# Attention with windows of three blocks: TensorE's step in another order (one piece for the q and k projection, the turned blocks in two pairs)

## The reference

```
qkv = xn @ Wqkv + bqkv            # 16 heads of 32, blocks of 128 tokens
scores = q @ kwin.T * 512 ** -0.5 # kwin: own block, the one before, the one behind
mask: |kpos - qpos| <= 128, and inside the sequence
attn = softmax(scores); out = attn @ vwin
x + out @ Wout + bout + ffn(xn)
```

## Time and profile before

| | before |
|---|---|
| median of 3 runs | 2508.47 us (2508.38 to 2508.74) |
| profiled execution | 2504.68 us |
| its span | 2502.9 us |
| PE busy | 2440.0 us, 97% |
| PEld, DVE, ACT, POOL busy | 80%, 64%, 58%, 14% |
| mean granted clock | 0.988 |

### The profile page before, as it was taken

How to read it: one execution, slowest core, us unless ns; L and a number is a source line. 1 busy time by engine, 2 the same in 40 slices (tenths; PEclk the granted TensorE clock), 3 DMA queues, 4 the chain that set the end, 5 groups by cost and what they waited for, 6 DMA issues and landing times.

```text
span 2502.9 us, 57228 instructions
## 1 busy us (share of the span) xinstructions
PE 2440.0 (97%) x20272; PEld 2001.1 (80%) x20272; DVE 1607.0 (64%) x4455; ACT 1460.3 (58%) x3748; POOL 339.2 (14%) x595
## 2 busy tenths in 40 slices
PE   6999999999999999989999999999999999999996
PEld 4788888888888888867888888888888888888885
DVE  5455555454555555436777777777777777777774
ACT  6333333333333333337777777777777777777774
POOL 0011111111111111010111111111111111111111
PEclk7999999999999999999999999999999999999998
DMA  4643334444443334324777777877787877777775
GB/s 159 206 110 110 108 108 114 117 117 117 117 116 105 111 109 112 101 68 124 203 200 198 199 199 203 201 200 200 195 203 203 200 199 198 202 197 196 201 191 148
DMA packets 653630, 398.24 MB, mean 159 GB/s; under 512 B 26032, under 2 KB 608688, under 8 KB 652896
## 3 DMA queue, kind: packets, MB, share of 16 engines
q1 hardware_dynamic: 653264, 395.15, 59.6%
q0 software_dynamic: 144, 0.17, 0.0%
HBM read 212.77 MB, written 182.45 MB: 158 GB/s over the span
## 4 chain that ended last, share of the span: by engine, by line
PE 48%; DMA 2%; ACT 2%; issue 1%; DVE 1%; SPq 0%; POOLq 0%; POOL 0%; ACTq 0%; DVEq 0%
PE job_ps L1203 13%; PE job_ps L1212 7%; PE job_ps L1221 7%; PE pT_ps L1288 7%; PE job_ps L1316 7%; PE score_ps L1274 7%; ACT wqkv_raw L1006 1%; DMA turned_blocks<-wqkv_raw 1%; DMA wqkv_raw<-turned_blocks 1%; PE pT_ps L1293 1%; ACT pT L1016 1%; SPq L916 0%; DVE wqkv_raw L1107 0%; PE score_ps L1326 0%; PE job_ps L1336 0%
## 5 line engine op out<-in xcount | busy, mean ns | idle before, releaser
L1006 ACT ACTIVATE wqkv_raw<-wqkv_raw,neg_max 128x384 f32<-128x384 f32 (+1 forms) x1024 | 619.7, 607 | 331.2 <-DVE neg_max L1090 331.1
L521 ACT ACTIVATE relu<-up_ps,fc_scale 128x512 f32<-128x512 f32 x256 | 176.1, 688 | 631.1 <-PE up_ps L663 631.1
L1090 DVE CUSTOM_DVE_ANT_0 wqkv_raw<-score_ps,mask 128x384 f32<-128x384 f32 (+1 forms) x1024 | 503.2, 547 | 5.1 <-PE score_ps L1274 3.3
L607 DVE SCALAR_TENSOR_TENSOR sq<-up_ps,relu 128x512 f32<-128x512 f32 x256 | 177.1, 692 | 495.7 <-ACT relu L521 494.9
L675 PE MATMUL down_ps<-proj_T,sq_lo 128*128 128x512 f32 x1024 | 404.8, 395 | 0.0
L673 PE MATMUL down_ps<-proj_T,sq_hi 128*128 128x512 f32 x1024 | 404.3, 395 | 0.3 <-DVE sq_lo L590 0.2
L659 PE MATMUL up_ps<-f_xT_hi,fc_T 128*128 128x512 f32 x1024 | 399.4, 390 | 1.4 <-DVE low L578 1.4
L661 PE MATMUL up_ps<-f_xT_lo,fc_T 128*128 128x512 f32 x1024 | 399.6, 390 | 0.0
L1203 PE MATMUL job_ps<-xT_hi,wqkv_hi 128*128 128x256 f32 x1024 | 329.2, 321 | 0.1
L1107 DVE STREAM_TRANSPOSE wqkv_raw<-wqkv_raw 128x384 f32<-128x384 f32 (+1 forms) x512 | 278.2, 562 | 45.6 <-ACT wqkv_raw L1006 42.1
L1203 PE MATMUL job_ps<-xT_hi,wqkv_lo 128*128 128x256 f32 x1024 | 288.5, 282 | 0.0
(11 more groups left out here) (130 smaller groups left out, 4262.7 us busy)
## 6 DMA issues: line engine op xcount, KB each, us to landing
turned_blocks<-wqkv_raw SPq DMA_DIRECT2D x124, 768.0 KB, 4.7
wqkv_raw<-turned_blocks SPq DMA_DIRECT2D x496, 192.0 KB, 3.6
xT_hi<-xT SPq DMA_DIRECT2D x65, 256.0 KB, 4.7
xT_lo<-xT SPq DMA_DIRECT2D x65, 256.0 KB, 4.8
f_x_in<-in_L_attn_x SPq DMA_DIRECT2D x256, 64.0 KB, 1.8
xT<-f_xT_hi SPq DMA_DIRECT2D x64, 256.0 KB, 3.0
xT<-f_xT_lo SPq DMA_DIRECT2D x64, 256.0 KB, 3.1
part_in<-in_L_attn_x SPq DMA_DIRECT2D x64, 256.0 KB, 5.2
```

The source lines that it names most:

```text
L521: nc.scalar.activation(relu[:, s % 2, :], up_ps[:, s % 2, :], ACT.Relu, scale=fc_scale2[:, s:s + 1]).then_inc(relu_done, 1)
L607: nc.vector.scalar_tensor_tensor(sq[:, s % 2, :], up_ps[:, s % 2, :], 0.0, relu[:, s % 2, :], ALU.max, ALU.mult).then_inc(sq_done, 1)
L1006: nc.scalar.activation(probs[:, u, cols], probs[:, u, cols], ACT.Exp, bias=neg_max[:, u:u + 1], scale=-1.0, accum_out=prob_sum[:, u:u + 1] ...
L1090: nc.vector.tensor_tensor_reduce(out=probs[:, u, cols], in0=score_ps[:, h, cols], in1=mask[:, cols], scale=-SCORE_SCALE, scalar=3e38, op0= ...
```

## The change

TensorE's step is put in another order: scores of block 0; heads 0 and 1 turned; all of the q and k projection; scores of block 1; heads 2 and 3 turned; the value product, block 0 first and block 1 behind it; the other projection. The transposes of the widened inverse sums go from heads 2 and 3 to heads 0 and 1, and the wait for them with these, and `scale_oT` reads them there. The value product waits for the moved blocks (`blocks_moved`) first, and for the copies of the turned heads (`pT_done`) only before its second half. ScalarE copies heads 0 and 1 each before the exp of the same number, and makes `qk_high` before it copies heads 2 and 3. GpSimd's wait before it overwrites `rcp_wide` is for the first two heads turned instead of all four. No instruction is added or taken away: the number of matmuls, copies and transfers is the same.

```
--- before.py
+++ after.py
@@ -960,7 +960,7 @@
             def widen_inverse_sums(t, b):
                 pool.wait_ge(rcp_done, 2 * t + b + 1)
                 if t >= 1:
-                    pool.wait_ge(turned, HC * t)
+                    pool.wait_ge(turned, HC * (t - 1) + 2)
                 heads = slice(b * HC, (b + 1) * HC)
                 nc.gpsimd.tensor_copy(rcp_wide[:, b, :, :], sum_rcp[:, heads].unsqueeze(2).to_broadcast([P, HC, DH])
                                       ).then_inc(rcp_widened, 1)
@@ -1009,7 +1009,7 @@
             def copy_pT(t, h):
                 i, _ = where(t)
                 seen = blocks_seen(i, 1)
-                last = 4 if h >= HC - 2 else seen.stop
+                last = 4 if h < 2 else seen.stop
                 act.wait_ge(turned, 4 * t + h + 1)
                 if t >= 1:
                     act.wait_ge(oT_scaled, t)
@@ -1057,18 +1057,18 @@
                 if b and b[0] == "v":
                     take_v(b[1], b[2], B_NUMBER[t - 1], b_bank(t - 1))
                 for h in range(HC // 2):
+                    if 1 <= t <= STEPS:
+                        copy_pT(t - 1, h)
                     if t < STEPS:
                         exp(t, 0, h)
-                    if 1 <= t <= STEPS:
-                        copy_pT(t - 1, h)
                 for h in range(HC // 2, HC):
                     if t < STEPS:
                         exp(t, 0, h)
+                if job_a(t) is not None:
+                    qk_high(job_a(t), A_NUMBER[t], a_bank(t))
                 for h in range(HC // 2, HC):
                     if 1 <= t <= STEPS:
                         copy_pT(t - 1, h)
-                if job_a(t) is not None:
-                    qk_high(job_a(t), A_NUMBER[t], a_bank(t))
                 for h in range(HC):
                     if t < STEPS:
                         exp(t, 1, h)
@@ -1114,7 +1114,7 @@
                     dve.wait_ge(oT_done, t)
                 nc.vector.tensor_tensor(oT.rearrange("p (b t) -> p b t", t=P),
                                         job_ps[:, pv_bank(t), 0:T].rearrange("p (b t) -> p b t", t=P),
-                                        pT[:, HC - 2:HC, 3, :], ALU.mult).then_inc(oT_scaled, 1)
+                                        pT[:, 0:2, 3, :], ALU.mult).then_inc(oT_scaled, 1)
 
             def oT_low(t):
                 dve.wait_ge(oT_hi_done, t + 1)
@@ -1222,7 +1222,7 @@
                                             w[:, k, :], start=(n == 0), stop=(n == PASSES * DC - 1))
                 return last
 
-            QUARTERS = 4
+            PARTS = 2
 
             def run_a(t, part):
                 u = job_a(t)
@@ -1233,9 +1233,9 @@
                     wait_job_bank(pe, 3 * t)
                     if c == 0:
                         pe.wait_ge(x_here[i % XR], 64 * (1 + i // XR) + (32 if i % XR == XR - 1 else 0))
-                each = 2 * PASSES * DC // QUARTERS
+                each = 2 * PASSES * DC // PARTS
                 last = project_qk(u, a_bank(t), part * each, (part + 1) * each)
-                if part == QUARTERS - 1:
+                if part == PARTS - 1:
                     last.then_inc(job_filled, 1)
 
             def run_b(t, part):
@@ -1249,9 +1249,9 @@
                         pe.wait_ge(oT_done, 4 * i + 4)
                     if kind == "out" and i == 0 and r == 0:
                         pe.wait_ge(wout_lo_done, 1)
-                each = PASSES * DC // QUARTERS
+                each = PASSES * DC // PARTS
                 last = (project_v if kind == "v" else project_out)(i, r, b_bank(t), part * each, (part + 1) * each)
-                if part == QUARTERS - 1:
+                if part == PARTS - 1:
                     last.then_inc(job_filled, 1)
 
             def scores(t, b):
@@ -1287,11 +1287,10 @@
                 for w in blocks_seen(i, 1):
                     last = nc.tensor.transpose(pT_ps[:, h % 2, w * P:(w + 1) * P], probs[:, u, w * P:(w + 1) * P],
                                                ident[:, :])
-                if h >= HC - 2:
-                    place = h - (HC - 2)
+                if h < 2:
                     pe.wait_ge(rcp_widened, 2 * t + 2)
                     last = nc.tensor.transpose(pT_ps[:, h % 2, 3 * P:4 * P],
-                                               rcp_wide[:, at(i, place), :, :].rearrange("p h t -> p (h t)"), ident[:, :])
+                                               rcp_wide[:, at(i, h), :, :].rearrange("p h t -> p (h t)"), ident[:, :])
                 last.then_inc(turned, 1)
 
             def probs_times_values(t):
@@ -1300,10 +1299,11 @@
                 wait_job_bank(pe, 3 * (t + 1) + 1)
                 if c == 0:
                     pe.wait_ge(v_done, min(2 * i + 3, NBLK))
-                pe.wait_ge(pT_done, HC * (t + 1))
-                for b in (1, 0):
+                for b in range(2):
                     if b == 0:
                         pe.wait_ge(blocks_moved, 16 * STRIPS * (t + 1))
+                    else:
+                        pe.wait_ge(pT_done, HC * (t + 1))
                     seen = blocks_seen(i, b)
                     for w in seen:
                         blk = 2 * i - 1 + b + w
@@ -1351,15 +1351,18 @@
             for t in range(STEPS + 3):
                 if t < STEPS:
                     scores(t, 0)
-                for part in range(QUARTERS):
-                    if 1 <= t <= STEPS:
-                        turn_probs(t - 1, part)
-                    run_a(t, part)
+                if 1 <= t <= STEPS:
+                    turn_probs(t - 1, 0)
+                    turn_probs(t - 1, 1)
+                run_a(t, 0)
+                run_a(t, 1)
                 if t < STEPS:
                     scores(t, 1)
                 if 1 <= t <= STEPS:
+                    turn_probs(t - 1, 2)
+                    turn_probs(t - 1, 3)
                     probs_times_values(t - 1)
-                for part in range(QUARTERS):
+                for part in range(PARTS):
                     run_b(t, part)
```

7 lines of the change are left out of this document (3 added, 4 removed).

## The result

The changed kernel takes 2516.89 us (median of 6 runs, 2511.74 to 2521.44), the kernel before, run beside it, 2508.43 us (2505.07 to 2509.30). The ratio is 1.0041, with a 95% interval of 1.0030 to 1.0051: slower by 0.4%, clear of noise. The forecast was 2524.5 us in a range from 2499 to 2545. (The sum's term for the last steps is -1.4 us, as in the paragraph on the rivals.)

What follows compares the result with a forecast made beforehand. TensorE's own sequence, busy for 97% of the span, was taken as the bound. Steps of 10.72 to 10.73 us against 10.59, over 124 steps, and the last steps gave +16 us: median 2524.5 us, range 2499 to 2545.

Steps and rivals of the forecast that it cites:

- The sum's term for the last steps: Last two attention steps, with no projection between: waits for copies shrink, between -3 and +1 us, taken as -1.4.
- TensorE's sequence, 10.35 + X, X = 0.20: Attention step without waits, 10.55 us; X is the seam from the last transpose to the value product, between 0.11 and 0.27.
- Three waits go: TensorE's waits for late copies before the value product, for k_lo (about 0.11 us each), and for copies freeing transpose banks vanish.
- The wait for T3's copy, 0.07: Value product's second half waits 0.07 us a step for ScalarE's copy of the last turned head, ending at 6.75.
- The widened sums, at nothing: Second block's inverse sums, needed earlier by heads 0 and 1's transposes, cost nothing: ready at 10.2, needed at 11.7 us.
- The transfer, 0.08: Value product's first half waits 0.08 us a step for the moved blocks, landing at 5.84 on average, needed at 6.14.
- The sum: Attention steps of 10.72 to 10.73 us against 10.59: +0.14 us a step, +17.4 us over 124 steps.
- The signs of being right: New profile: steps near 10.65 us, no k_lo wait, copy wait in most steps, transfer wait in a third, value product at 6.1.
- From the profiled run to the median: Whole kernel: median taken 3.8 us above the profiled run, as in the kernel before, so 2520.7 became 2524.5 us.
- the transfer as the bound: Rival: moved blocks' transfers land 0.3 us later and pace the attention steps, +37 us, 2545 us; chance 0.14.
- The gain: Rivals with copies and transfers in time: little gain, 2505 us, chance 0.16; or faster, 2493 us, chance 0.17.

Runs made afterwards that it cites:

- experiment 2: Changed kernel with the value product's block 0 half reading constant weights, so TensorE does not wait for the moved blocks' transfer: 2498.62 us, ratio 0.9978.
- Experiment 4: Kernel before, with VectorE's addition of the output projection put behind the first two of block 0's four maxima: 2485.53 us, ratio 0.9923.
- experiment 7: Kernel of experiment 2 with heads 2 and 3 turned ahead of the second scores, one change of shape less: 2476.70 us, ratio 0.9890.
- Experiment 1: Changed kernel with the value product's halves in their old order, waiting for the copies ahead of both: 2596.89 us, ratio 1.0372.
- experiment 9: Changed kernel with both loads of x put a step later on SP's queue, ahead of the four transfers in: 2537.74 us, ratio 1.0138.

## Why the prediction was right

- *TensorE's sequence, 10.35 + X, X = 0.20.* Right. X is 0.20 (0.202 to 0.211 for the middle half of the steps). The step of experiment 2 is 10.613 with 0.037 of wait for the copy in it, so 10.576, against 10.57. The gathered projection saves nothing, as worked out.
- *Three waits go.* Right: k_lo and the copies leave TensorE idle no longer. Experiment 4 prices what stood behind them, VectorE's late maxima, at 0.166 us a step. The step is still not shorter than the mean of before, because the sixth change of shape takes 0.148 back (experiment 7) and T3's copy 0.037; the net is the 0.019 of experiment 2. The Trainium skill ("TensorEngine Tiling (Array Packing)", Key Properties) says that a change of tiling mode drains the engine; a price of that kind is what the runs show, though not that it is a drain. One reading of the earlier trace rows in the prediction was wrong, without a part in the sum: the two rows for k_lo are 108 waits in 112 steps and 0.25 us each, not 54 and 0.11. They are idle time of weight loads. From starts, they cost TensorE 0.13 us in a long step and nothing in a short one.
- *The wait for T3's copy, 0.07.* Mis-sized: 0.037. The copies came when I said, 1819.65 is 6.79 into the step against 6.75 (a copy follows a copy at 0.40, not at 0.36, which was an exp behind a copy). But I added the 0.14 us from copy to matmul of the earlier trace rows, and it was 0.05. Experiment 1 shows that both are real; the last section says what decides between them.
- *The widened sums, at nothing.* Right in the steps, no wait. At the very end TensorE is idle for them twice, 0.8 us together.
- *The transfer, 0.08.* The step in which the loss lies; 0.11 (experiment 2), and the bounds of 0 to 0.25 held it. That it came so near is partly luck. I had a mean landing of 5.84 us and a spread of 0.4; in the changed kernel the mean is 5.54 and the spread (standard deviation) 0.7. The earlier mean makes the wait shorter, the wider spread longer, and the two misses nearly cancel.
- *The sum.* +0.131 a step against +0.14: 0.03 too much for the copy and 0.03 too little for the transfer, which cancel. From the first step's start to the hundred and twenty-fifth's it is 16.0 us against 17.4; the end gains 2.4 against 1.4, and the untouched stage ahead took 1.7 more in this execution.
- *The signs of being right.* Two of five came, the other projection free of k_lo and the wait for the copy in most steps, of which only the 0.05 to the matmul tells. The other three did not. The four kinds of step take 10.61 to 10.82 us, not all near 10.65 (which didn't fit my own sum of 10.72 either). The transfer is late in 28 of 112 steps, a quarter and not a third, and the value product starts at 6.27 in the mean, not at 6.1.
- *From the profiled run to the median.* The weak place. I added the 3.8 us by which the median of before lay above its profiled run. For the changed kernel the median lies 3.2 below its profiled run. Single runs of it spread over 10 us. Without the wait for the transfer nine runs spread over 4.6 (experiment 2), so most of the spread hangs on when transfers land. And the 3.8 us were no fixed distance: in the experiments the medians of the kernel before, 2504.1 to 2507.3, lay between 0.6 below and 2.7 above its profiled run. So the forecast is 8 us above the median and 1 us from the profiled run.

Of the rivals, the transfer as the bound was right in place and too high in size. It took landings 0.3 us later than those of before, and they came 0.3 earlier. A late step does give the next transfer room: behind one the blocks land 5.32 into the step in the mean, else 5.62. But that is not why they were early, for in experiment 2, where no step is late, the mean is 5.54 too. The gain did not come, although without the transfer's wait there was one (experiment 2, ratio 0.9978).

What stays open is why the same transfer lands anywhere from 4.5 to 6.7 us into the step (nine steps of ten), and why it lands 0.3 us earlier in the mean in the changed kernel than before. The loads of x make it some 0.5 us longer in the steps that have one; the rest was not taken apart.

## What to carry to other kernels

An order that saves an engine's waits can be paid for by whoever is needed earlier: list for each block not only what it waits for but how much room each of its inputs has, and look at the spread of a transfer's landing, not only its mean. Before reordering the engine that is full, look for the short instruction of another engine that stands in front of its inputs: moving one addition behind two maxima gave 0.8%, more than any complete kernel with TensorE in another order. And count changes of array shape in a loop; joining two pieces of the same shape was worth 0.9% where TensorE had no wait for the transfer, a fifth of it a wait for a copy that went with it.

## What was not expected of the hardware

- What a wait costs TensorE behind its release depends on which instruction waits. Where the wait is an instruction of its own ahead of the weight load (0.051 us long, line 1303 below), it is 0.104 us from the signal to the weight load and 0.135 to the matmul. Where the weight load carries the wait itself, it is 0.042 and 0.044. The first form stands where the value product opens, the second before its second half in the changed kernel; that is the 0.14 and the 0.05.
- It is not the change of shape that decides. The other projection of the kernel before comes behind matmuls of another shape and starts 0.06 after k_lo's end (1831.10 + 0.47 to 1831.63, below; the weight load waits). The projection that waits for x in experiment 9 comes behind transposes of its own shape and takes 0.135 (a wait of its own).

```profile
L1303 PEldq EVENT_SEMAPHORE  x111: 51/51/51, 1268.8 to 2434.6; - x111
...
1831.10 0.47 DVE L1132 SCALAR_TENSOR_TENSOR k_lo<-job_ps,qk_bias,k_hi 128x256 fp32r<-128x256 f32 x1
...
1831.63 0.51 PE L1221 MATMUL job_ps<-wout_hi,oT_hi 128*128 128x512 f32 x1
```

- One change of shape less in a step, with the same instructions, made it 0.148 us shorter (experiment 7 without its 0.037 us for the copy).
